# A learned extra key as a 126th row of the first key chunk, and the first queries split ahead of the last projection

## The reference

```python
kh = jnp.concatenate([kh, jnp.broadcast_to(bias_k, (b, 1, H, K))], axis=1)
vh = jnp.concatenate([vh, jnp.broadcast_to(bias_v, (b, 1, H, K))], axis=1)
logits = jnp.einsum('bqhk,bthk->bhqt', qh, kh) / scale
weights = jax.nn.softmax(logits, axis=-1)
ctx = jnp.einsum('bhqt,bthk->bqhk', weights, vh).reshape(b, q_len, H * K)
return ctx @ wo + bo
```

## Time and profile before

| | us |
|---|---|
| three runs | 1279.06, 1282.16, 2014.25 |
| median | 1282.16 |
| the profiled execution | 1280.71 |
| its span | 1278.9 |
| mean granted TensorE clock | 0.996 |

### The profile page before, as it was taken

The page is one execution under the profiler, slowest core; times in us unless marked ns, Lnnn a source line. Parts: engine busy times, 40 slices in busy tenths (PEclk is TensorE's granted clock), DMA queues, the critical chain, the costliest instruction groups (busy, mean ns, idle before and its releaser), DMA issues.

```text
span 1278.9 us, 26549 instructions
## 1 busy us (share of the span) xinstructions
PE 1252.2 (98%) x8140; PEld 1152.3 (90%) x8140; DVE 794.6 (62%) x1369; ACT 807.2 (63%) x1585; POOL 905.1 (71%) x750
## 2 busy tenths in 40 slices
PE   6999999999999999999999999999999999999998
PEld 6779999999999999998887999999999999999897
DVE  5745656566666666566785656666656666655654
ACT  4745666666656566676584656666666666666755
POOL 4737777777777777678673768686868686866882
PEclk9999999999999999999999999999999999999999
DMA  5401111111111111012331111111111111101131
GB/s 166 144 10 49 37 61 36 60 36 60 36 60 36 60 37 59 31 39 83 121 126 40 38 38 61 36 60 36 60 36 60 36 60 37 60 30 52 50 95 40
DMA packets 30670, 72.58 MB, mean 57 GB/s; under 512 B 3104, under 2 KB 4512, under 8 KB 30624
## 3 DMA queue, kind: packets, MB, share of 16 engines
q1 hardware_dynamic: 30336, 71.49, 18.1%
q10 hardware_dynamic: 288, 0.52, 0.1%
HBM read 71.52 MB, written 0.48 MB: 56 GB/s over the span
## 4 chain that ended last, share of the span: by engine, by line
PE 91%; DVE 4%; ACT 2%; issue 2%; DMA 0%; POOL 0%; DVEq 0%; ACTq 0%; SPq 0%; POOLq 0%
PE psum L682 36%; PE psum L703 13%; PE psum L704 13%; PE psum L705 13%; PE psum L650 5%; PE psum L747 4%; PE psum L714 2%; PE psum L671 2%; DVE g_prod L1193 1%; PE psum L689 1%; PE psum L696 1%; PE psum L600 1%; DVE qh L1222 1%; ACT on L994 1%; DMA w_raw<-weights 0%
## 5 line engine op out<-in xcount | busy, mean ns | idle before, releaser
L509 POOL TENSOR_TENSOR pt<-slots,pt 125x512 fp32r<-125x512 f32 (+1 forms) x384 | 446.4, 1168 | 216.5 <-ACT slots L988 184.9
L682 PE MATMUL psum<-qs,ctx 128*125 128x384 f32 (+1 forms) x2304 | 543.1, 372 | 1.3 <-ACT slots L1019 0.8
L682 PEld LDWEIGHTS psum<-qs,ctx 128*125 128x125 f32 x2304 | 396.4, 187 | 47.5 <-ACT slots L1019 8.3
L703 PE MATMUL psum<-ctx,pt 125*128 125x258 f32 x1344 | 385.5, 287 | 2.8 <-ACT on L994 2.7
L704 PE MATMUL psum<-ctx,pt 125*128 125x256 f32 x1344 | 379.3, 282 | 0.0
L705 PE MATMUL psum<-ctx,pt 125*128 125x258 f32 x1344 | 379.1, 282 | 0.0
L1281 DVE TENSOR_TENSOR t_max<-psum,t_max 125x512 f32<-125x512 f32 (+1 forms) x320 | 199.2, 622 | 261.2 <-PE psum L682 260.9
L987 ACT ACTIVATE pt<-slots 125x512 fp32r<-125x512 f32 (+1 forms) x384 | 221.1, 576 | 193.1 <-DVE slots L1269 178.6
L1019 ACT ACTIVATE slots<-psum 125x512 f32<-125x512 f32 (+1 forms) x384 | 207.0, 540 | 141.8 <-DVE t_max L1281 132.2
L703 PEld LDWEIGHTS psum<-ctx,pt 125*128 125x128 f32 x1344 | 253.4, 189 | 19.9 <-ACT on L994 12.7
L704 PEld LDWEIGHTS psum<-ctx,pt 125*128 125x128 f32 x1344 | 254.1, 189 | 6.0
(11 more groups left out here) (104 smaller groups left out, 1062.2 us busy)
## 6 DMA issues: line engine op xcount, KB each, us to landing
nat_stage<-ctx_nat SPq DMA_DIRECT2D x64, 375.0 KB
tr_stage<-ctx_tr SPq DMA_DIRECT2D x64, 375.0 KB, 3.0
w_raw<-weights SPq DMA_DIRECT2D x70, 256.0 KB, 2.7
dk_rest<-dk_rows SPq DMA_DIRECT2D x2, 768.0 KB, 6.3
w_raw<-weights ACTq DMA_DIRECT2D x2, 256.0 KB, 4.2
dk_first<-dk_rows SPq DMA_DIRECT2D x2, 256.0 KB, 4.5
xres<-x_rows SPq DMA_DIRECT2D x4, 112.0 KB, 4.3
out_rows<-xres SPq DMA_DIRECT2D x4, 112.0 KB, 1.9
```

The costliest lines, as they stand in the source:

```text
L509: nc.gpsimd.tensor_tensor(split_weights(h, LO, c), slot(h, c), as_f32(split_weights(h, HI, c)), ALU.subtract).then_inc(pt_lo, 1)
L682: last = mm(scores(h, k), ctx_tr_chunk(half, a, c), qs[h][:, m, half, 0:R], start=(half, a, m) == terms[0], stop=(half, a, m) == terms[-1])
L703: mm(out_bank[:, 0:D + 2], hi, ctx_nat_hi(c), start=(c == 0), stop=False, skip_group_check=True)
```

## The change

The 1500 keys stay 12 chunks of 125, and the extra key becomes row 126 (partition 125) of the first chunk: its logit stands in `t_max` for the maximum and in `slots` for the exponential, its weight goes with the others into the products. Its context row is zero, it has a one in the column of the sums, and a second column, zero for all other keys, sums its weight alone. Thus `lb`, `p_extra`, `den`, `mx_part`, `spread` with L826, the two small steps of `group_max` and ScalarE's exponential for the extra key are gone. The logits reach the row through DRAM: SyncE writes `lb_rows` to `lb_flat`, and two loads per half and batch bring a row of at most 512 numbers back. `extra_logits` moves behind the last `carried_queries`. ScalarE and VectorE split heads 0 to 14 of the first tiles before the last head is out, and the last head's columns by themselves; the first score takes its HI terms first and waits for HI and LO apart. ScalarE's normalisation waits for `pn_extra`, which is now made between the reciprocal and VectorE's share.

```diff
+XT = CT + 1
 NCT = T // CT
...
-SPREAD = TQ - 1
+LAST_HEAD = (H - 1) * TQ
...
-        slots = [sb("slots0", [CT, NCT, GT[0] * P], F32)]
+        slots = [sb("slots0", [XT, NCT, GT[0] * P], F32)]
         at_slots1 = place_at[0]
-        slots.append(sb("slots1", [CT, NCT, GT[1] * P], F32))
...
-        t_max = [sb(f"t_max{h}", [CT, GT[h] * P], F32) for h in range(HALVES)]
-        pt = sb("pt", [CT, 2, RING, GT[0] * P], F32R)
+        t_max = [sb(f"t_max{h}", [XT, GT[h] * P], F32) for h in range(HALVES)]
+        pt = sb("pt", [XT, 2, RING, GT[0] * P], F32R)
...
+        def keys_of(c):
+            return XT if c == 0 else CT
...
-            return ctx[0:CT, at:at + D + 2]
+            return ctx[0:keys_of(c), at:at + D + 2]
...
-            return ctx[0:CT, at:at + D]
+            return ctx[0:keys_of(c), at:at + D]
...
         def slot(h, c):
-            return slots[h][:, c, :]
+            return slots[h][0:CT, c, :]
+        def logits(h, c):
+            return slots[h][0:keys_of(c), c, :]
         def split_weights(h, part, c):
-            return pt[:, part, c % RING, 0:GT[h] * P]
+            return pt[0:keys_of(c), part, c % RING, 0:GT[h] * P]
         def scores(h, k):
             return S_BANK[k % 2][0:CT, 0:GT[h] * P]
-        def shift(h):
-
-            return NB_BANK[0:CT, 0:GT[h] * P]
+        def shift(h, c):
+            return NB_BANK[0:keys_of(c), 0:GT[h] * P]
+        def most_heads(ap):
+            return ap.rearrange("p (n r) -> p n r", r=P)[:, :, 0:LAST_HEAD]
+        def last_head(ap):
+            return ap.rearrange("p c (n r) -> p c n r", r=P)[:, :, :, LAST_HEAD:P]
...
-            sp.dma_start(spread[:], spread_in).then_inc(consts_in, 16)
...
+                def extra_row(b, h):
+                    return lb_flat[l:l + 1, ds(b * FLAT + h * GT[0] * P, GT[h] * P)]
+                def load_extra(b, h, first):
+                    if not first:
+                        sp.wait_ge(mt_mm, INIT + l * GROUPS + b * 2 + (h - 1))
+                        settle(sp)
+                    sp.dma_start(t_max[h][CT:XT, :], extra_row(b, h)).then_inc(max_row_in[h], 16)
+                    if not first:
+                        sp.wait_ge(pt_lo, INIT + l * LAYER_STEPS + b * STEPS + (h * NCT - STEPS + 1))
+                        settle(sp)
+                    sp.dma_start(slots[h][CT:XT, 0, :], extra_row(b, h)).then_inc(slot_row_in[h], 16)
                 def batch_loads(b, first, last):
                     nat, tr = l * (B * PIECES) + b * PIECES, l * (B * PIECES) + b * PIECES + PIECES
+                    if not first:
+                        load_extra(b, 1, False)
                     if not last:
                         load_tr(b + 1, tr, 0)
                     if not first:
-                        for p in range(1, PIECES):
+                        for p in range(1, PIECES - 1):
                             load_nat(b, nat + p, p)
+                    if not last:
+                        load_extra(b + 1, 0, False)
+                    if not first:
+                        load_nat(b, nat + PIECES - 1, PIECES - 1)
                     if not last:
                         load_tr(b + 1, tr + 1, 1)
                         load_nat(b + 1, nat + PIECES, 0)
                         for p in range(2, PIECES):
                             load_tr(b + 1, tr + p, p)
+                sp.wait_ge(lb_rows_ready, INIT + l + 1)
+                sp.dma_start(lb_flat[l:l + 1, :].rearrange("a (n h e) -> (a h) n e", h=H, e=TQ),
+                             lb_rows[:].rearrange("h (n e) -> h n e", e=TQ)).then_inc(lb_written, 16)
+                sp.wait_ge(lb_written, l * 16 + 16)
+                for h in range(HALVES):
+                    load_extra(0, h, True)
...
-            nat_ones = ctx[0:CT, N_TR:N_TR + N_NAT].rearrange("p (t d) -> p t d", t=NCT)[:, :, D:D + 2]
-            nc.gpsimd.memset(as_f32(nat_ones), 1.0).then_inc(setup_step, 1)
+            nat = as_f32(ctx[:, N_TR:N_TR + N_NAT]).rearrange("p (t d) -> p t d", t=NCT)
+            pool.wait_ge(setup_step, INIT + 1)
+            settle(pool)
+            nc.gpsimd.memset(nat[96:P, 0, :], 0.0).then_inc(setup_step, 1)
             pool.wait_ge(setup_step, INIT + 2)
+            settle(pool)
+            nc.gpsimd.memset(nat[:, :, D:D + 2], 1.0).then_inc(setup_step, 1)
+            pool.wait_ge(setup_step, INIT + 3)
+            settle(pool)
+            nc.gpsimd.memset(nat[0:CT, :, D + 1], 0.0).then_inc(setup_step, 1)
...
                 R = GT[h] * P
                 terms = [(half, a, m) for half in range(DC) for a, m in TERMS]
+                if first_of is not None:
+                    terms = [(half, a, m) for m in (HI, LO) for half in range(DC) for a in (HI, LO)[:2 - m]]
                 for half, a, m in terms:
-                    if first_of is not None and (a, m) == TERMS[0]:
-                        pe.wait_ge(first_qs_lo, INIT + first_of * DC + half + 1)
+                    if first_of is not None and (half, a) == (0, HI):
+                        pe.wait_ge(first_qs_lo if m else first_qs_hi, INIT + first_of + 1)
                     last = mm(scores(h, k), ctx_tr_chunk(half, a, c), qs[h][:, m, half, 0:R],
                               start=(half, a, m) == terms[0], stop=(half, a, m) == terms[-1])
                 last.then_inc(s_mm, 1)
...
                 for j in range(GT[h]):
-                    last = nc.tensor.transpose(MT_BANK[:, j * CT:(j + 1) * CT], t_max[h][:, j * P:(j + 1) * P],
-                                               ident[0:CT, 0:CT])
+                    last = nc.tensor.transpose(MT_BANK[:, j * XT:(j + 1) * XT], t_max[h][:, j * P:(j + 1) * P],
+                                               ident[0:XT, 0:XT])
...
                 for j in range(GT[h]):
-                    last = nc.tensor.transpose(NB_BANK[0:CT, j * P:(j + 1) * P],
-                                               mx_group[:, j:j + 1].to_broadcast([P, CT]), ident[:])
+                    last = nc.tensor.transpose(NB_BANK[0:XT, j * P:(j + 1) * P],
+                                               mx_group[:, j:j + 1].to_broadcast([P, XT]), ident[:])
...
-                        if last_quad and u == 3:
-                            extra_logits()
...
-                pe.wait_ge(consts_in, 16 * N_CONSTS)
-                pe.wait_ge(lb_rows_ready, INIT + l + 1)
-                pe.wait_ge(qp_out, INIT + l * (2 * H) + 2 * (H - 1))
-                settle(pe)
-                by_query = lb_rows[:].rearrange("h (t e) -> h t e", e=TQ)
-                for j in range(TQ):
-                    at = SPREAD - j
-                    last = mm(bank[6][:, 0:NT], spread[:, at:at + P], by_query[:, :, j],
-                              start=(j == 0), stop=(j == TQ - 1))
-                last.then_inc(lb_spread, 1)
+                extra_logits()
                 pe.wait_ge(tr_lo, INIT + l * (B * PIECES) + PIECES)
...
+                            pe.wait_ge(max_row_in[1 - h], (l * B + (b if h else b - 1)) * 16 + 16)
...
+                pe.wait_ge(consts_in, 16 * N_CONSTS)
...
+                        if last_quad and u == 3:
+                            act.wait_ge(qp_out, INIT + l * (2 * H) + 2 * (H - 1))
+                            act.wait_ge(gp_used, INIT + (l + 1) * H)
+                            for half in range(DC):
+                                go(most_heads(qs[0][:, HI, half]), most_heads(qt_flat[:, half, 0:GT[0] * P]),
+                                   ACT.Copy).then_inc(most_qs_hi, 1)
...
                 act.wait_ge(qp_out, INIT + (l + 1) * (2 * H))
-                act.wait_ge(gp_used, INIT + (l + 1) * H)
-                for half in range(DC):
-                    go(qs[0][:, HI, half], qt_flat[:, half, 0:GT[0] * P], ACT.Copy).then_inc(first_qs_hi, 1)
-                act.wait_ge(lb_ready, INIT + l + 1)
+                go(last_head(qs[0][:, HI]), last_head(qt_flat[:, :, 0:GT[0] * P]), ACT.Copy).then_inc(first_qs_hi, 1)
...
-                    act.wait_ge(rden_ready, INIT + l * GROUPS + b * 2 + (h + 1))
+                    act.wait_ge(pn_ready, INIT + l * GROUPS + b * 2 + (h + 1))
...
+                            if first and k == NCT:
+                                act.wait_ge(lb_written, l * 16 + 16)
...
-                        if c == 1 and (h == 1 or not first) and not (tail and h == 1):
-                            act.wait_ge(px_ready, INIT + group)
-                            at = tiles_of(b - 1 if h == 0 else b, 1 - h)
-                            go(p_extra[:, at], p_extra[:, at], ACT.Exp).then_inc(pe_done, 1)
...
+                for half in range(DC):
+                    dve.wait_ge(most_qs_hi, INIT + l * DC + half + 1)
+                    V.tensor_tensor(most_heads(qs[0][:, LO, half]), most_heads(qt_flat[:, half, 0:GT[0] * P]),
+                                    most_heads(as_f32(qs[0][:, HI, half])), ALU.subtract)
+                dve.wait_ge(first_qs_hi, INIT + l + 1)
```

(30 more changed lines are left out.)

50 lines of the change are left out of this document (23 added, 27 removed).

## The result

The changed kernel took 1273.45 us (median of 6, 1272.31 to 1276.31), the kernel before 1281.51 in the same runs: ratio 0.9946, interval 0.993 to 0.9962. A second series gave 1274.01 us and 0.9957 (0.9944 to 0.997). Forecast were 1274.5 us and a gain of 6.15. The ratios leave out the executions that lie far above all others of their kernel (2014 us for the one before), and they come with the measurement: quotients of the medians differ from them by up to 0.0009 (0.9937 in the first series).

A forecast was written before the change was run, and what follows sets the result against it. The prediction took TensorE, 91% of the span in the last-ending chain, as the bound. Gains of 2.75 us (first scores earlier) and 3.4 (no half clock) sum to 6.15; 1280.7 - 6.15 = 1274.5 us, range 1270.5 to 1282.

The forecast's parts named there:

- handover: From the projections to the first score, once a layer: scores start 1.34 and 1.41 us earlier, together 2.75 us.
- batches: Attention batches: shorter steps on VectorE and ScalarE lie beside TensorE's work, so no gain was taken.
- clock: Behind the first score: no fall to half clock once the narrow matmuls go, 1.7 us a layer, together 3.4 us.
- Two chains, both to be cut: Before the first score: TensorE's matmuls and the queries' chain are equally long; removing one alone gives 0.2 us.
- the queries' chain: Before the first score: ScalarE copies head 15 out and splits the first queries, then VectorE subtracts.
- What is late next: At the first score: TensorE waits for GpSimd's last transposed keys, ending at 62.42 and 680.81 us.
- Contention: Before the first score: VectorE's new subtractions meet GpSimd's step; 0.5 us taken, bounds 0 and 1.3.
- the rival: Before the first score: the subtractions hold GpSimd for their full length, scores 1.3 us later, 1276.1 us; chance 0.12.
- the 2.7 that the prediction named as a sign: In the batches: TensorE's wait for ScalarE's normalised contexts was to be near 2.7 us in total.
- The rival of the stretched product: Ahead of ScalarE's normalisation: pn_extra, if still stretched by 0.3 us, costs 30 groups 9 us, 1283.5 us; chance 0.08.
- SyncE: Logits' write and row loads through DRAM: in by about 70 us, first used not before 79.8, so no cost.

The follow-up runs named there:

- row_only: Changed kernel with the logits back ahead of the last projection and the queries' split back behind the last head: 1280.81 us, ratio 1.0006 to the kernel before.
- split_only: Kernel before with only the queries of 15 heads split ahead of the last projection; logits and narrow matmuls stay: 1279.75 us, ratio 1.0005.
- pieces: Changed kernel with TensorE waiting for the first batch's transposed keys chunk by chunk, not for all ahead of the first score: 1273.47 us, ratio 0.9958.
- narrow_back: Changed kernel with 16 narrow fp32 matmuls, result unused, put back between the logits and the first score: 1277.26 us, ratio 0.9975.
- row_wide: row_only with 10 wide matmuls, result unused, put into TensorE's idle time ahead of the first score: 1277.15 us, ratio 0.9983.

## Why the prediction was right

*The time.* 1273.45 us lies in the range and 1.05 below the point. The gain adds up differently than forecast: handover 3.3 us (forecast 2.75), batches 1.7 (0.9 a layer at like clock, row_only against before; forecast 0), clock 0.0016 of the mean, 2.0 us (forecast 3.4). That is 7.0, against the 5.5 and 6.9 of the two ratios. That the point came so near is in part luck: the clock was booked 1.4 too high and the batches 1.7 too low.

*Two chains, both to be cut*: shown. row_only keeps 5.26 us and split_only 5.03. But of the queries' chain the split ahead is the smaller part: without it the handover is 3.98 us, since the logits' new place alone lets the last head out earlier.

*What is late next*: GpSimd's keys, as said, with TensorE waiting 0.40 and 0.43 us. pieces took that wait away and won 0.5 us a layer.

*Contention*: 0.5 us was assumed, 0.25 measured, so the step was mis-sized. The mechanism is the one of the rival. VectorE's first subtraction went first and held GpSimd, the second was held by GpSimd and took 1.97 us for 0.68. The Trainium skill ("SBUF — State Buffer", Who interferes with whom) says that the one that starts first blocks the other, and the traces agree, in both orders. What was wrong in the rival's sum is that the hold is at most what is left of the first instruction when the other becomes ready: 0.25 us of 0.39 here.

*The clock*: the fall behind the first score is gone, as forecast, but the reason was wrong. narrow_back has the narrow matmuls and no fall, row_only has none of them and falls, and the mean clocks over 11 runs each (0.9972 and 0.9948) say the same. And 3.4 us were booked as if the other falls stood still; the mean over the runs gives 2.0. row_wide shows that unfilled idle time ahead of the score brings a fall. What brought it in the kernel before and in split_only, where TensorE was busy but with narrow work on both sides of the last projection, stays open: narrow_back has as much narrow work, in one piece, and did not fall. No run separates the order from the rest.

*The batches*: the step that failed, at nothing instead of 1.7 us. I compared the lengths of the steps ahead of ScalarE and not the start of the first, which is worth 0.25 us a layer; the other 0.6 us a layer stay open. TensorE's waits for ScalarE even grew, 2.7 to 3.2 us, against the 2.7 that the prediction named as a sign. The rival of the stretched product did not come: with its input from PSUM it takes 160 to 165 ns in all 32.

*SyncE* cost nothing. The last of the first row loads is issued at 69.0 us, the first transposes that read a row start at 84.0, and no wait of TensorE names them.

## What to carry to other kernels

Where two chains of like length end at one point, cut either and the profile shows a new idle time of the same size; a change that is worth something only as a whole should be judged as a whole. Idle time of TensorE that looks free can cost clock afterwards: filling 2.1 us of it with useless matmuls won 3 us here. Judge a clock effect by the mean over many runs, since a fall that is gone in one place can stand in another. And in a wait that the critical engine sits behind, count the register instructions between the wait and the first step: 0.1 us each here.

## What the runs showed of the hardware

- Falls of the clock last 3.4 us each at 0.50 and moved about: in the changed kernel's profiled execution near 10, 40 and 634 us, in the one before near 10, at 64.7 and at 682.5, and there with no idle time of TensorE over 0.23 us ahead of the last two. Single runs of one kernel had means from 0.992 to 0.999 (row_only), 7 us apart.
- A VectorE subtraction with two SBUF inputs and a GpSimd one exclude each other: whichever comes second is held for part of what is left of the first. GpSimd took 1.76 for 1.51 us, two VectorE steps 2.53 and 1.54 us where their like took 1.29.
- A register instruction on VectorE's queue between a wait and the step behind it costs about 0.1 us: 0.52, 0.42 and 0.32 us from TensorE's product to VectorE's step with two, one and none.
- A row copied through DRAM, written in pieces of 32 bytes at 65.94 us, had landed 2.2 us later (the first row load, which waits for it, is issued at 68.14).
